# Attention steps on TensorE one at a time, or two together: an eight-core transformer kernel

## What is computed

```python
# layer 0 attention (causal); q and k from low-rank and rotary projections, then gelu
scores = einsum('bhqd,bhkd->bhqk', q, k) / sqrt(64)
scores = where(causal, -inf, scores)
out = einsum('bhqk,bhkd->bhqd', softmax(scores), v) @ wo + bo
# layer 0 feed-forward: gelu(x @ ternary(W_fc)) -> layernorm -> @ ternary(W_proj)
# layer 1 attention (not causal); q and k pass a spectral filter
out = einsum('bhqk,bhkd->bhqd', softmax(q k^T / sqrt(64)), v) @ w_out + b_out
# layer 1 feed-forward: a tree picks one of 16 leaves for q, k and v of each token,
# then full attention of width 1024 over the tokens
```

## Time and profile before

| | us |
|---|---|
| Median of 3 runs | 4948.01 (4946.77 to 5389.83) |
| Profiled execution | 4945.06 |
| Its span, first to last instruction (core 7, the slowest) | 4943.5 |
| Spans of the eight cores | 4922.7 to 4943.5 |
| TensorE busy, share of the span | 4549.8, 92% |
| ScalarE busy | 2494.5, 50% |
| VectorE busy | 2291.2, 46% |
| GpSimd busy | 1112.4, 23% |

### The profile page before, as it was taken

How to read it: one execution, slowest core, us unless ns; L and a number is a source line. 1 busy time by engine, 2 the same in 40 slices (tenths; PEclk the granted TensorE clock), 3 DMA queues, 4 the chain that set the end, 5 groups by cost and what they waited for, 6 DMA issues and landing times.

```text
span 4943.5 us, 56754 instructions; the slowest of 8 cores (4922.7 to 4943.5 us)
## 1 busy us (share of the span) xinstructions
PE 4549.8 (92%) x20820; PEld 1770.3 (36%) x20820; DVE 2291.2 (46%) x3857; ACT 2494.5 (50%) x2891; POOL 1112.4 (23%) x1124
## 2 busy tenths in 40 slices
PE   6788879999999999999998899899999999999999
PEld 3222234444422223444443223344442222244444
DVE  5887755544113344344465544555511234343445
ACT  4577743222398886122225787233229988812220
POOL 1067733322111100023010101334321110002300
PEclk9798999999999999999999999999999999999999
DMA  7656554333223322422161122433311112233002
GB/s 189 190 189 192 182 181 147 114 117 97 54 45 82 70 81 63 120 52 44 62 175 43 44 63 92 160 111 118 111 41 31 33 54 79 58 94 88 26 35 94
DMA packets 319034, 471.86 MB, mean 95 GB/s; under 512 B 177902, under 2 KB 217008, under 8 KB 308528
## 3 DMA queue, kind: packets, MB, share of 16 engines
q1 hardware_dynamic: 291248, 427.60, 28.2%
q0 software_dynamic: 27520, 40.64, 5.2%
HBM read 384.00 MB, written 99.09 MB: 98 GB/s over the span
## 4 chain that ended last, share of the span: by engine, by line
PE 76%; DVE 11%; DMA 4%; ACT 3%; issue 3%; POOL 3%; SPq 0%; DVEq 0%; ACTq 0%; POOLq 0%
PE pall L190 75%; ACT arena L201 3%; DVE arena L217 3%; DVE arena L204 2%; DVE arena L214 2%; POOL arena L204 1%; DVE cols L221 1%; DMA arena<-l0f_w2T 1%; POOL arena L208 1%; DVE cols L541 1%; DVE cols L543 1%; DVE arena L720 1%; DMA arena<-l_wkr 1%; DMA arena<-w_scr 1%; DMA arena<-x_in 1%
## 5 line engine op out<-in xcount | busy, mean ns | idle before, releaser
L190 PE MATMUL pall<-arena 128*128 128x512 bf16 (+3 forms) x20668 | 4536.3, 381 | 359.2 <-DVE arena L204 101.6
L190 PEld LDWEIGHTS pall<-arena 128*128 128x128 bf16 (+3 forms) x20668 | 1757.1, 100 | 3130.9 <-issue 1598.7
L201 ACT ACTIVATE arena<-pall,cols 128x1024 bf16<-128x1024 f32 (+3 forms) x2096 | 1968.4, 1010 | 903.7 <-PE pall L190 883.8
L204 DVE TENSOR_TENSOR arena<-arena 128x512 f32<-128x512 f32 (+5 forms) x980 | 659.3, 678 | 825.4 <-ACT arena L201 663.8
L201 ACT ACTIVATE arena<-pall 128x512 bf16<-128x512 f32 (+3 forms) x480 | 312.7, 653 | 1265.8 <-PE pall L190 1260.4
L204 POOL TENSOR_TENSOR arena<-arena 128x512 f32<-128x512 f32 (+1 forms) x472 | 554.3, 1175 | 878.3 <-ACT arena L201 442.6
L204 POOL TENSOR_TENSOR cols<-cols 128x1 f32<-128x1 f32 (+2 forms) x282 | 191.2, 678 | 1763.4 <-DVE cols L208 1530.4
L217 DVE COPY arena<-pall 128x512 f32<-128x512 f32 (+1 forms) x226 | 146.0, 682 | 376.9 <-PE pall L190 376.8
L217 DVE CAST arena<-pall 128x512 bf16<-128x512 f32 (+1 forms) x160 | 118.6, 741 | 413.5 <-PE pall L190 413.5
L217 POOL CAST arena<-arena 64x512 bf16<-64x512 f32 (+1 forms) x136 | 86.1, 633 | 912.7 <-DVE arena L217 733.5
L208 POOL TENSOR_SCALAR arena<-arena,cols 128x512 bf16<-128x512 f32 x128 | 222.8, 1752 | 33.2 <-DMA arena<-l0f_wfcT 16.3
(11 more groups left out here) (58 smaller groups left out, 569.8 us busy)
## 6 DMA issues: line engine op xcount, KB each, us to landing
arena<-wfc_scr SPq DMA_DIRECT2D x64, 1024.0 KB, 5.3
z_scr<-arena SPq DMA_DIRECT2D x96, 512.0 KB, 2.6
arena<-z_scr SPq DMA_DIRECT2D x96, 512.0 KB, 4.0
arena<-x_in SPq DMA_DIRECT2D x64, 512.0 KB, 5.5
arena<-l0f_wfcT SPq DMA_DIRECT2D x64, 512.0 KB, 4.9
arena<-l0f_w2T SPq DMA_DIRECT2D x64, 512.0 KB, 4.5
arena<-wqf_scr SPq DMA_DIRECT2D x64, 256.0 KB, 2.6
arena<-sel_scr SPq DMA_DIRECT2D x32, 512.0 KB, 8.9
```

The costliest lines, as they stand in the source:

```text
L190: return self.pe.put(lambda e: e.matmul(out, lhsT, rhs, start=start, stop=stop), after, signal)
L201: lambda e: e.activation(out, in_, func, bias=bias, scale=scale), after)
L204: return q.put(lambda e: e.tensor_tensor(out, a, b, op), after)
```

## The change

The loop over the steps goes over pairs of steps. `emit_s` is cut in two: the matmuls stay, the exp becomes `emit_exp`. A pair puts in S(i), exp(i), S(i+1), then the masks and the product of step i-2, exp(i+1), the product of step i-1, and both ticks. The masks of query blocks 1 to 3, which were put in one step after their scores, are now put in with the next pair. Instructions, shapes and buffers stay the same.

```diff
+    s_tok = {}
+
     def emit_s(i):
...
         k.last_qk = tok
+        s_tok[i] = tok
+
+    def emit_exp(i):
+        qb, c, kt, off, last = steps[i]
+        s = sbank[i % 2]
+        tok = s_tok.pop(i)
         j = i % 3
         src = v3(k.ps(s[0].idx, 2), 2, 512)[:, :, off:512]
         dst = pt[j][:, :, off:512]
...
-    for i in range(len(steps)):
+
+    for i in range(0, len(steps), 2):
         emit_s(i)
-        if i >= 1 and steps[i - 1][0]:
-            emit_mask(i - 1)
-        if i >= 2:
+        emit_exp(i)
+        emit_s(i + 1)
+        if i:
+            for j in (i - 2, i - 1):
+                if steps[j][0]:
+                    emit_mask(j)
             emit_pv(i - 2)
-        if state["late"]:
-            emit_recip()
-        rs, rb = rate(steps[i][0], i, causal and steps[i][2] >= 4 * steps[i][0])
-        k.tick(0.55 + 0.55 * (512 - steps[i][3]) / 512, rs, rb)
+        emit_exp(i + 1)
+        if i:
+            emit_pv(i - 1)
+        for j in (i, i + 1):
+            if state["late"]:
+                emit_recip()
+            rs, rb = rate(steps[j][0], j, causal and steps[j][2] >= 4 * steps[j][0])
+            k.tick(0.55 + 0.55 * (512 - steps[j][3]) / 512, rs, rb)
+    emit_mask(len(steps) - 2)
     emit_mask(len(steps) - 1)
     emit_pv(len(steps) - 2)
     emit_pv(len(steps) - 1)
```

## The result

The changed kernel takes 4,995.1 us (median of 5, four of them between 4,988.0 and 4,996.1) against 4,948.01; the ratio is 1.0094, 95% interval 1.0080 to 1.0108. It is slower by 47 us: clear of noise, but less than the 2% from which on two kernels count as different. In some executions of any of these kernels the cores of one die run at a lower granted clock; all ratios here, and the times beside them, are of executions without that, and of old_paired_q_early, whose profile has it on cores 4 to 7, the cores 0 to 3 are read.

The account below looks back on a forecast made before the run. ScalarE was taken to bound attention steps without side work, TensorE those with it. Walk +90, copies' cover -53 and masks +6 gave +43 us on 4,945.06; with the median 2.95 higher, 4,990 us, range 4,950 to 5,040.

Parts of the forecast that it names:

- (1): TensorE's order: two turns between 64-row and 128-row matmuls a pair, not four; -0.20 us a pair where TensorE bounds.
- (5): S(i+1) right behind S(i) on TensorE: 0.22 us taken, upper end 0.39; 0.32 would add 8 us.
- part (3): Second loop through scores and exps: 1.98 us a pair plus 0.108 per side matmul; mixed sequences walked, +90 us in all.
- (2): New loop through TensorE's order, exp(i+1) waiting for V(i-2): 2.21 us a pair, +0.21 without side work.
- The walk: Both orders carried step by step through the four passes: +14, +30, +18 and +28 us without bank copies.
- Rival A: Steady-state prices hold in all four passes because side work comes in long bursts: 4,925 us, chance 0.17.
- (4): At changes of head pair, side work and scores cover the bank copies: -53 us, bounds 0 and -60.
- (6): Causal passes, query blocks 1 to 3: masks issued behind two steps' side work on VectorE; +6 us, bounds -10 and +50.
- rival C: First pass: each of 96 diagonal pairs pays a 1.08 us mask wait, +104 us, 5,090 us; chance 0.14.
- (7): Two portions of side work meet without attention between them: no gain or loss, bounds -5 and +10 us.
- the signs named ahead: Trace marks of being right: 2.2 us pairs, late second scores, line 217 near zero, passes of 447, 618, 364, 622 us.
- signs of being wrong: Exps still every 1.00 us, TensorE's line 204 wait over 80 us, or other stages changed by over 5 us.

Follow-up runs that it names:

- old_paired_q_early: Old order with side work after every second step, masks ahead of it, and block 2's query projection moved to block 0 in the non-causal passes; ratio 0.9981 to before.
- pairs_4buf: The changed kernel with a fourth exp buffer in place of the second staging buffer of the bank copies; 4,950 us, ratio 1.0004 to before.
- old_order_side_first: The kernel before, with that step's side work put ahead of the first V product of each head pair; ratio 0.9986 to before.
- old_order_ticks_paired: The kernel before, with both portions of side work put in after every second step; ratio 1.0002 to before.

## Why the prediction was right, point by point

4,990 us was forecast, 4,995.1 measured. The main mechanism, the new wait for V(i-2), was right and tested by itself. That the sum also came out is in part luck: the first pass was forecast 14 us too low and the other three together 14 too high.

- **(1) and (5), turns.** Right for the turn, too large for what it saves. The second score can follow 0.23 us behind the first (0.22 was taken), and a pair with four side matmuls then takes 2.38 us (2.41 forecast). But that is under half of them: on average those pairs take 2.73 us for 2.78, 0.05 less where 0.17 was forecast, and pairs with six 3.12 for 3.02, where 0.20 less was forecast. In the others the second score is late behind an exp, which part (3) has as the effect of mixed sequences.
- **(2), the loop through V(i-2).** Right in place and size: 2.23 us for 2.21, and 2.01 when the fourth buffer takes it away. The walk gave 55 us for it over four passes (as worked out for pairs_4buf), the runs give 49. The Trainium skill's rule that matmuls stay in program order ("TensorE: Matmul & The Clock Gate", Step-by-step: what each phase is for) goes with it: V's weights load 0.35 us behind every late score load shown.
- **(3), the walk in mixed sequences.** +14 and +14 for passes two and four; +13 and +8 measured. It carried the old side work over as it was. For the third pass it is off: +9 against +2. Rival A, the steady prices, gives +11 less 16 for the second pass and is refuted by it, at +13.
- **(4), cover for the copies.** The waits on line 217 fell by 38 us in passes two to four (14.3 and 1.9 in the fourth), and the first pass's wait for ScalarE's copy by 15; forecast were 39 and 15 us of time. But a wait that is gone isn't time won: in old_order_side_first 8.0, 2.7 and 5.6 us less waiting in these passes gave 6, 0 and 5 us, and in old_order_ticks_paired 6.8, 5.7 and 6.2 us less went with 3, 4.5 and 10 us. In the changed kernel itself no run shows what the cover is worth.
- **(6), masks.** The mis-sized step: +6 forecast, and 13 us come back in the first pass when the masks go ahead of the side work, 6 in the third. In the first the wait on line 204 had risen with the change, from 43.2 to 56.3. In the third it had fallen, so that "in the third pass nothing is lost" may stand, and the 6 us may be a gain open to the old order too. It is the mechanism of rival C at a fifth of its price: 19 us over 96 pairs, 0.20 each and not 1.08. C charged every pair with a whole wait as if the old order had none; it had 40 of them already.
- **(7), two ticks in a row.** "No gain or loss found" was wrong for the first pass: collecting the side work costs 21 us there in the old order, and some 11 in the new one with four buffers and early masks, just over the bound of 10. In the other passes it gave time back.
- By passes: forecast -1, +14, +9, +14 and +6 for masks; measured +19, +13, +2, +8. The stages outside the passes differ by under 3 us each on core 7, apart from the stretch ahead of the first pass, 193.2 us for 188.4 at a clock of 0.91 (0.94 before) with code that is the same; over the eight cores its median is 186 us and was 187.

Of the signs named ahead, these came: pairs of 2.2 us with 0.11 us of idle time ahead of an exp, the second score load late, line 217 near zero, and windows of 618, 358 and 617 us for 618, 364 and 622. The first window did not, 460 for 447 (by its own terms, 440.6 + 14 - 15 + 6, it should have read 446). None of the signs of being wrong came: line 204 stayed under 80 us.

Open: why the walk is too dear by some 7 us in the third pass and 6 in the fourth. It already fell 21 us short of the old order in the third, and what those waits become in the new one was not tried.

## What to carry to other kernels

An order on an in-order engine saves what its turns cost only where that engine bounds in that very step; here that was 0.2 us in the best pairs, and 0.05 on average over the 62 pairs of the second pass with four side matmuls. Before grouping steps, follow every buffer once around the new loop: with three buffers the group of two waited for its own product, with four it didn't, and the same order went from 0.9% slower to level, and to 0.4% faster with the masks put ahead of the side work. Grouping also collects what hangs on the loop (masks, side work, copies); look at each for whose queue it now stands in front of.

## What the runs showed of the hardware

Two pairs of 64-row matmuls for four different banks run one behind the other without a turn's price: their four weight loads are one group of 0.17 us at 1607.89, and the pair with its eight 128-row matmuls is 2.38 us. Ten times 0.216 (two pairs of scores, eight others) is 2.16, so the two turns cost 0.11 us each, as they did around a single step's scores.
An exp that can start at once behind its forerunner adds 1.00 to 1.01 us (26 in 26.25), one that starts on an idle engine 1.11 (the form). In the second pass of the changed kernel this holds for all 262 exps behind a gap, be it of 0.03 us or of 3.9, so a gap on ScalarE costs 0.11 us beside its own length.
